# A one-core Perceiver kernel: eight key groups of its second cross-attention computed at the end of the first one, and a state-space scan whose inputs come from ScalarE and whose states TensorE adds

## The chip, the cores and the metric

The kernel runs on one core of one Trainium2 chip. The metric is the device time of one execution in microseconds. Before the change the median of 3 runs is 1534.51 us, from 1531.64 to 1535.97.

## The reference, cut to what matters

`x` is 128 rows of 256 numbers. Six layers are added to it in turn, each on the layer norm of what came before.

```python
x = x + _L0_xattn_ref(_layernorm(x), ctx_1024, Wq, Wkv, Wo, bo)     # 16 heads, 12544 context rows
x = x + _L0_attn_ref(_layernorm(x), ...)                             # banded self-attention
x = x + _L0_ffn_ref(_layernorm(x), ...)                              # 8 experts, top 2
x = x + _L1_xattn_ref(_layernorm(x), ctx_1024, mask, W, b)
x = x + _L1_attn_ref(_layernorm(x), ...)                             # scan
x = x + _L1_ffn_ref(_layernorm(x), ...)                              # 32 experts, top 8
```

The fourth layer makes its keys from the same context rows as the first, with one head, and the keys are the values too:

```python
q = relu(input @ W.T + b); k = relu(context @ W.T + b)
probs = softmax(where(mask, -inf, q @ k.T)); out = probs @ k
```

The fifth, with 256 channels and 16 states (`n`) per channel, sums over the 128 rows with cumulative sums:

```python
log_dA = clip(delta * A, -7, 20); log_R = cumsum(log_dA)
S = cumsum(delta * B * x * exp(min(-log_R, 20)))
y = sum over n of C * exp(log_R) * S, + x * D
```

## The kernel before, in words

Each layer is a stage with one instruction block per engine. Engines wait for each other through semaphores; a stage begins when every engine has left the stage before. The order on each engine is written out by hand. Layer norm is shared (`norm_vector`, `norm_pool`, `norm_tensor`, L97 to L121). `spin` (L123) issues matmuls of the identity on itself, whose result nobody reads; each float32 matmul is two MATMUL records with two weight loads.

**The context stage** (`stage_context`, L181) walks 14 chunks of 896 context rows through 16 heads: 224 steps. In step `u` TensorE turns the probabilities of head `u` (L620), turns the output of step `u - 2` (L562), on odd steps makes two heads' scores (L555), in seven of eight steps makes a value tile (L544), makes a key piece for step `u + 4` (L533) and multiplies the probabilities of step `u - 1` with the values (L575). ScalarE copies the turned probabilities (L396), then the value tile (L402), then exponentiates the next step (L378, L380). VectorE takes the low parts, maxima and running sums. GpSimd splits value tiles (L317, L318) and, once per chunk, the context chunk after next into a high float32r part and a low rest (`split_context`, L295 and L297). The last eight steps make no value tiles, the last four no key pieces. After step 223 TensorE projects the heads with `wo` (L588), in parts, since the last sums arrive last.

**The band stage** (`stage_band`, L1560) is the second layer. While it runs, SyncE loads what the later stages need (L1599 to L1613), one context chunk among it. **`stage_mix0`** (L1418) is the third: a router chain of small VectorE operations (L1459 to L1469) beside the experts on TensorE (L1531, L1540). GpSimd splits the relu stage's weight `wx` and context chunk 0 meanwhile (L1443 to L1450).

**The relu stage** (`stage_relu_context`, L1066) is the fourth. A chunk's keys are four groups: `relu_keys` (L1390) is six float32r matmuls of 448 columns (L1401) into bank `G % 2`, and ScalarE adds the bias and the relu (L1189). VectorE casts a group to its high part (L1258), GpSimd takes the low part (L1162). TensorE turns the keys (L1316), makes the scores (L1328, L1333), turns the probabilities (L1374) and sums (L1344). Group 0 to 3 are made ahead (`done = [4]`), and rounds 0 to 12 make four groups each, those of the next chunk. ScalarE splits the high part of a context chunk (L1196), GpSimd the low part (L1157). The keys `d_kT` have a ring of two chunks.

**The scan stage** (`stage_scan`, L842) works in four blocks of 64 channels by 16 states, 1024 columns. VectorE and GpSimd make the products with `ea` (L972, L909), GpSimd makes the inputs `g` (L900), TensorE takes cumulative sums with a triangle (L1044, L1053), ScalarE exponentiates (L929, L932), VectorE multiplies (L989, L996) and adds the 16 states of each channel (L997). **`stage_mix1`** (L675) is the sixth layer and begins with `spin(8, 0)`.

## Time and profile before

| | |
|---|---|
| median of 3 runs | 1534.51 us |
| the profiled execution | 1531.62 us |
| its span | 1529.9 us |
| TensorE matmuls busy | 96% |
| VectorE busy | 71% |
| ScalarE busy | 54% |
| GpSimd busy | 39% |
| mean granted clock of TensorE | 0.987 |

The profiled execution took 1.7 us more than its span, which is what lies around the instructions. Shares are means over stages with different limits. A timeline row gives the start from the span's start in us, the duration in us (of all instructions of a merged row together), the engine, the line, what is written and read, the shape, the count, and in brackets the idle time of the engine before it with what ended it. PE is TensorE, PEld its weight loads, DVE VectorE, ACT ScalarE, POOL GpSimd. A duration reported for a group counts its tail, so successive starts say better what an instruction costs in a stream.

### The profile page before, as it was taken

Reading aid. Unit: us, or ns where it says so; the run is one execution under the profiler, and the core shown is the slowest. Engines: PE = TensorE matmul, PEld = TensorE weight load, DVE = VectorE, ACT = ScalarE, POOL = GpSimd, SP = SyncE. Lnnn points to the kernel's source line nnn. Section 1 sums busy time; section 2 is a strip of 40 time slices with the busy share of each in tenths; the row PEclk is TensorE's granted clock in tenths of the full one; section 3 lists DMA queues with packets and bytes.
Section 4 is the critical chain, followed back from the end, with each engine's and each line's share of the span. In section 5 each row is a group of like instructions: output and inputs, shape, how many; then the busy total and the mean of one; then the engine's idle time right before and its main releaser. Section 6 shows DMA issues by size and latency. Waiting matters only on the chain. (4 is left out here: it accounts for less than half of the span.)

```text
span 1529.9 us, 24927 instructions
## 1 busy us (share of the span) xinstructions
PE 1467.8 (96%) x9257; PEld 1272.2 (83%) x9257; DVE 1084.1 (71%) x2051; ACT 832.6 (54%) x1581; POOL 598.7 (39%) x517
## 2 busy tenths in 40 slices
PE   8999999999999999999999999999987979999769
PEld 6888888888888888888888888888875869999648
DVE  5777777777777777777777777777787337777784
ACT  4555566556555565556656566556652136666221
POOL 5243433434343434343434343343310245666240
PEclk9999999999999999999999999999999799999899
DMA  5000000000000000000000000000004221221720
GB/s 186 1 25 1 1 25 1 25 1 25 1 25 1 25 1 25 1 25 1 25 1 20 6 1 25 1 1 1 1 28 179 83 105 55 82 82 34 302 104 4
DMA packets 11099, 58.92 MB, mean 39 GB/s; under 512 B 2330, under 2 KB 4707, under 8 KB 9956
## 3 DMA queue, kind: packets, MB, share of 16 engines
q1 hardware_dynamic: 10980, 57.33, 10.0%
q8 instruction: 75, 1.23, 0.3%
q14 instruction: 44, 0.36, 0.1%
HBM read 57.19 MB, written 0.13 MB: 37 GB/s over the span
## 5 line engine op out<-in xcount | busy, mean ns | idle before, releaser
L487 DVE TENSOR_TENSOR pT<-ps,pT 128x896 fp32r<-128x896 f32 x224 | 244.5, 1091 | 203.8 <-ACT pT L396 203.8
L317 POOL CAST V<-Vraw 128x512 fp32r<-128x512 f32 x189 | 115.7, 612 | 651.1 <-ACT Vraw L402 550.5
L396 ACT ACTIVATE pT<-ps 128x896 fp32r<-128x896 f32 x224 | 205.9, 919 | 179.4 <-PE ps L562 178.6
L402 ACT COPY Vraw<-ps 128x512 f32<-128x512 f32 x189 | 110.9, 587 | 266.0 <-PE ps L544 266.0
L318 POOL TENSOR_TENSOR V<-Vraw,V 128x512 fp32r<-128x512 f32 x189 | 242.7, 1284 | 15.1
L433 DVE TENSOR_REDUCE nmx<-ps 128x1 f32<-128x896 f32 x224 | 242.0, 1080 | 0.0
L380 ACT ACTIVATE prob<-ps,nm 128x896 f32<-128x896 f32 x224 | 223.8, 999 | 0.0
L620 PE MATMUL ps<-ident,prob 128*128 128x128 f32 x1568 | 214.2, 277 | 8.7 <-ACT prob L380 4.5
L575 PEld LDWEIGHTS ps<-pT,V 128*128 128x128 f32 x1568 | 215.0, 188 | 8.1 <-issue 0.3
L575 PE MATMUL ps<-pT,V 128*128 128x256 f32 x1568 | 220.3, 280 | 0.0
L620 PEld LDWEIGHTS ps<-ident,prob 128*128 128x128 f32 x1568 | 167.5, 140 | 17.0 <-ACT prob L380 9.2
L441 DVE TENSOR_REDUCE osb<-ps 128x128 f32<-128x256 f32 x224 | 95.0, 424 | 89.2 <-PE ps L575 80.0
L544 PE MATMUL ps<-wvh,cTh 128*128 128x512 f32 x392 | 141.8, 443 | 1.1 <-DVE V L477 1.1
L426 DVE TENSOR_TENSOR Kl<-ps,Kh 128x448 fp32r<-128x448 f32 x224 | 137.4, 614 | 1.8 <-ACT Kh L371 1.8
L533 PE MATMUL ps<-cTh,wkh 128*128 128x448 f32 x448 | 131.0, 373 | 6.5 <-DVE Kl L426 2.3
L533 PE MATMUL ps<-cTh,wkl 128*128 128x448 f32 x448 | 128.4, 368 | 0.5 <-DVE wkl L464 0.5
L533 PE MATMUL ps<-cTl,wkh 128*128 128x448 f32 x448 | 128.2, 367 | 0.4 <-DVE cTl L461 0.4
L544 PE MATMUL ps<-wvh,cTl 128*128 128x512 f32 x392 | 123.1, 395 | 0.0
L544 PE MATMUL ps<-wvl,cTh 128*128 128x512 f32 x392 | 122.6, 394 | 0.0
L371 ACT CAST Kh<-ps 128x448 fp32r<-128x448 f32 x224 | 118.5, 529 | 1.7 <-PE ps L533 1.5
L533 PEld LDWEIGHTS ps<-cTh,wkh 128*128 128x128 f32 x448 | 81.5, 188 | 30.8 <-DVE Kl L426 12.7
L555 PE MATMUL ps<-Kh,qh 64*128 64x448 f32 x448 | 94.0, 415 | 0.0
(312 smaller groups left out, 2426.7 us busy)
## 6 DMA issues: line engine op xcount, KB each, us to landing
raw<-in_ctxT SPq DMA_DIRECT2D x14, 896.0 KB, 4.4
d_raw<-in_ctxT SPq DMA_DIRECT2D x14, 896.0 KB, 4.6
w<-in_w SPq DMA_DIRECT2D x2, 4096.0 KB, 18.1
wg<-in_wg SPq DMA_DIRECT2D x1, 4352.0 KB, 17.8
wu<-in_wu SPq DMA_DIRECT2D x1, 4352.0 KB, 27.6
wd<-in_wd SPq DMA_DIRECT2D x1, 4352.0 KB, 36.3
e_ea<-in_alog SPq DMA_DIRECT2D x1, 2048.0 KB, 7.8
d_mrow<-in_mask SPq DMA_DIRECT2D x14, 112.0 KB, 4.5
```

Of the source, the lines that this page charges most:

```text
L317: link(pool, nc.gpsimd.tensor_copy(v_high(g, i), by_head(Vraw[:, j % 2, :])), "pool_chain")
L318: nc.gpsimd.tensor_tensor(v_low(g, i), by_head(Vraw[:, j % 2, :]), v_high(g, i).bitcast(F32), ALU.subtract).then_inc(sem("v_split"), 1)
L371: nc.scalar.copy(Kh[:, slot, cols], ps[:, piece_bank(p), 0:HK]).then_inc(sem("kh_ready"), 1)
L380: nc.scalar.activation(prob[:, :, :], S[u % 2], ACT.Exp, bias=nm[:, par, h:h + 1], scale=1.0, accum_out=rs[:, b:b + 1]).then_inc(sem("exp_ ...
L396: nc.scalar.activation(pT[u % 2][:, :, 0, :], pT_ps, ACT.Copy).then_inc(sem("pTh_ready"), 1)
L426: nc.vector.tensor_tensor(Kl[:, slot, cols], ps[:, piece_bank(p), 0:HK], Kh[:, slot, cols].bitcast(F32), ALU.subtract).then_inc(sem("kl_re ...
L433: nc.vector.tensor_reduce(nmx[:, :], S[u % 2], mybir.AxisListType.XY, ALU.max, negate=True).then_inc(sem("chunk_max"), 1)
L487: nc.vector.tensor_tensor(pT[u % 2][:, :, 1, :], pT_ps, pT[u % 2][:, :, 0, :].bitcast(F32), ALU.subtract).then_inc(sem("pTl_ready"), 1)
L533: mm = nc.tensor.matmul(ps[:, piece_bank(p), 0:HK], w[:, k, m * P:(m + 1) * P], x[:, k, half * HK:(half + 1) * HK], start=(n == 0), stop=( ...
L544: mm = nc.tensor.matmul(ps[:, bank, :], x[:, k, i * P:(i + 1) * P], w[:, k, cols], start=(n == 0), stop=(n == 3 * KT - 1))
L575: mm = nc.tensor.matmul(OT_ps, V[g % 2][:, k, h % HG, :], pT[u % 2][:, k, :, :].rearrange("p a q -> p (a q)"), start=(k == 0), stop=(k == ...
L620: mm = nc.tensor.transpose(pT_ps[:, k, :], prob[:, :, :].rearrange("p a n -> p (a n)")[:, k * P:(k + 1) * P], ident[:, :])
```

## The change

It does these things:

- **Context stage.** SyncE loads `wx` into the first half of the value buffer and GpSimd splits it near the start. SyncE loads context chunks 0 and 1 once more after chunk 13; GpSimd splits the first as any chunk (at step 206) and the second in quarters after all value splits. In steps 216, 217, 218, 219, 222 and 223 TensorE makes one relu key group each in bank 6, and ScalarE relus it between the copy of the turned probabilities and the next exponential. Groups 6 and 7 follow in banks 2 and 3 amid the final projection.
- **Buffers.** `row0` and `dist` leave the lasting buffers; `tri` and `below` are made in `stage_mix0`; the `afc` load moves to the band stage. The key ring is four chunks, its first two shared with the context stage and with the scan.
- **Band and mix0.** Three runs of `spin(3, ...)` are added between the last matmuls of the band; the first spin of `stage_mix0` goes from 8 to 6. Context chunks 2 and 3 are loaded in the band stage, 4 and 5 in `stage_mix0`, whose GpSimd splits 2 and 3. VectorE's router selection waits for `below`.
- **Relu stage.** It starts at group 8, groups 8 to 12 are made ahead, rounds 0 to 8 make three groups, rounds 9 to 12 four. Chunk 0's casts come ahead of the query's, and its key turns ahead of groups 10 to 12.
- **Scan.** GpSimd makes three `ea` products instead of two and no inputs. ScalarE makes all inputs with 16 instructions of 256 elements, each written with a step of 16 elements. VectorE makes one product and no state sums; TensorE adds the states of a block with 16 matmuls of the identity on 64 columns that lie 16 elements apart, at the end.
- **mix1.** The first spin goes from 8 to 5.

```diff
+                def later_keys(G, bank):
+                    act.wait_ge(sem("dk_done"), G + 1)
+                    act.wait_ge(sem("wx_early"), 32)
...
@@ stage_context, TensorE @@
+                    if u in later_at:
+                        pe.wait_ge(sem("o_added"), u - 1)
+                        pe.wait_ge(sem("vraw_ready"), len(v_steps))
+                        later_keys(later_at.index(u), 6)
...
+                        if u in later_at:
+                            pe.wait_ge(sem("dkT_ready"), later_at.index(u) + 1)
                         weighted_sum(u - 1)
...
                         project(range(0, 4))
+                        later_keys(6, 2)
...
                 turn_heads((4, 5, 6), 7)
+                later_keys(7, 3)
@@ stage_relu_context @@
-    early, split = v["early_groups"], v["early_splits"]
-    ahead = v["groups_ahead"]
-    done = [max(early, ahead)]
+    early, done = 8, [13]
+    SKIP = 2
...
-        share = -(-(groups - done[-1]) // left) if left > 0 else 0
+        share = (groups - done[-1]) // left if left > 0 else 0
@@ stage_scan, ScalarE @@
+                for k in range(NST):
+                    ins = nc.scalar.activation(cn(g[:, :])[:, :, k], dx[:, :], ACT.Copy, scale=bc[:, k:k + 1])
+                ins.then_inc(sem("g_ready"), 1)
@@ stage_scan, VectorE @@
-                    nc.vector.tensor_reduce(y[:, n * BD:(n + 1) * BD], cn(la[n][:, :]), AX_X, ALU.add).then_inc(sem("y4_ready"), 1)
...
+                dve.wait_ge(sem("states_added"), NB)
+                nc.vector.tensor_tensor(res[:, :], res[:, :], ps[:, 0, 0:D], ALU.add).then_inc(sem("res_ready"), 1)
@@ stage_scan, TensorE @@
+                def add_states(n):
+                    pe.wait_ge(sem("y4_ready"), n + 1)
+                    pe.wait_ge(sem("neg_ready"), NB - 1)
+                    pe.wait_ge(sem("R_ready"), NB - 1)
+                    for k in range(NST):
+                        mm = nc.tensor.matmul(ps[:, 0, n * BD:(n + 1) * BD], v["ident"][:, :], cn(la[n][:, :])[:, :, k],
+                                              start=(k == 0), stop=(k == NST - 1))
+                    mm.then_inc(sem("states_added"), 1)
...
                     sums(n)
                     if n + 2 < NB:
                         log_R(n + 2)
+                    else:
+                        add_states(n - 2)
+                add_states(NB - 2)
+                add_states(NB - 1)
```

## Rows read from the trace of the kernel before

**Rows 1.** Timeline of TensorE, two successive rounds of the relu stage.

```profile
1266.67 1.07 PE L1344 MATMUL ps<-d_kNh,d_pTh 128*128 128x256 f32 x7
...
1269.26 0.57 PE L1401 MATMUL ps<-d_cTh,d_wxh 128*128 128x448 f32 x2
...
1274.13 0.92 PE L1374 MATMUL ps<-ident,d_prob 128*128 128x128 f32 x7
...
1281.65 0.63 PE L1401 MATMUL ps<-d_cTh,d_wxh 128*128 128x448 f32 x2
```

**Rows 2.** Timeline of TensorE, the relu stage before its first full round.

```profile
1240.09 0.65 PE L1401 MATMUL ps<-d_cTh,d_wxh 128*128 128x448 f32 x2
...
1249.52 0.69 PE L1316 MATMUL ps<-ident,d_kT 128*128 128x128 f32 x2 [4.50 <-DVE d_kNl L1263]
...
1259.13 0.67 PE L1401 MATMUL ps<-d_cTh,d_wxh 128*128 128x448 f32 x2 [2.06 <-ACT d_kT L1189]
```

**Rows 3.** Timeline of VectorE and GpSimd, the first chunk's casts and low parts.

```profile
1241.70 3.19 DVE L1258 CAST d_kTh<-d_kT 128x448 fp32r<-128x448 f32 x4
...
1242.16 4.80 POOL L1162 TENSOR_TENSOR d_kTl<-d_kT,d_kTh 128x448 fp32r<-128x448 f32 x4 [5.12 <-DVE d_kTh L1258]
```

**Rows 4.** Timeline of GpSimd in the context stage, around one chunk's split.

```profile
913.27 1.67 POOL L295 CAST cTh<-raw 128x1792 fp32r<-128x1792 f32 x1
...
920.85 0.61 POOL L317 CAST V<-Vraw 128x512 fp32r<-128x512 f32 x1 [1.78 <-ACT Vraw L402]
...
961.31 0.61 POOL L317 CAST V<-Vraw 128x512 fp32r<-128x512 f32 x1 [7.53 <-ACT Vraw L402]
```

**Rows 5.** Timeline of VectorE, steps 217 and 219, without value tiles.

```profile
1130.77 1.09 DVE L487 TENSOR_TENSOR pT<-ps,pT 128x896 fp32r<-128x896 f32 x1 [0.87 <-ACT pT L396]
...
1140.48 1.09 DVE L487 TENSOR_TENSOR pT<-ps,pT 128x896 fp32r<-128x896 f32 x1 [0.87 <-ACT pT L396]
```

**Rows 6.** Timeline of ScalarE and TensorE, the last two steps.

```profile
1155.46 0.28 ACT L378 ACTIVATE al<-nm 128x1 f32<-128x1 f32 x1
...
1159.53 1.99 PE L588 MATMUL ps<-wo,oT 128*128 128x256 f32 x8
...
1161.38 1.07 PE L575 MATMUL ps<-pT,V 128*128 128x256 f32 x7
```

**Rows 7.** Stretch: bounds, length, busy us per engine, clock, DMA share, GB/s.

```profile
1192.00:1196.00 4.00, 3.37 (x9) 2.28 (x10) 0.42 (x1) 0.00 (x0) 0.00 (x0) 0.50 0.47 146
```

**Rows 8.** Timeline of TensorE and VectorE in `stage_mix0`.

```profile
1197.82 3.76 PE L126 MATMUL ps<-ident 128*128 128x128 f32 x16 [0.78 <-PEq L1595]
...
1204.60 2.29 DVE L1463 TENSOR_SCALAR c_ex<-c_ex,c_one 128x8 f32<-128x8 f32 x1
...
1212.39 0.48 DVE L1481 SCALAR_TENSOR_TENSOR res<-ps,c_comb,res 128x256 f32<-128x256 f32 x1 [3.27 <-PE ps L1540]
```

**Rows 9.** Timeline of VectorE in the scan stage.

```profile
1457.38 2.94 DVE L989 TENSOR_TENSOR e_g<-e_g,e_inv 128x1024 f32<-128x1024 f32 x1
...
1473.96 1.22 DVE L997 TENSOR_REDUCE e_y<-e_la 128x64 f32<-128x1024 f32 x1
1475.21 0.42 DVE L1014 TENSOR_TENSOR res<-res,e_y 128x256 f32<-128x256 f32 x1
```

**Rows 10.** Timeline of TensorE: spins, narrow matmuls, a cumulative sum of the scan.

```profile
1178.80 2.17 PE L126 MATMUL ps<-ident 128*128 128x128 f32 x18
...
1185.49 1.93 PE L1742 MATMUL ps<-b_v,b_kx 128*128 128x16 f32 x16
...
1465.56 1.98 PE L1053 MATMUL ps<-e_g,tri 128*128 128x512 f32 x4 [1.49 <-DVE e_g L989]
```

**Rows 11.** Timeline of ScalarE in the scan stage.

```profile
1432.62 0.42 ACT L923 ACTIVATE e_u<-e_u 128x256 f32<-128x256 f32 x1 [11.59 <-DVE e_u L943]
```

**Rows 12.** Timeline of TensorE and VectorE at the start of `stage_mix1`.

```profile
1475.96 3.44 PE L126 MATMUL ps<-ident 128*128 128x128 f32 x16 [3.64 <-PEq L885]
...
1477.51 0.41 DVE L105 TENSOR_SCALAR xn<-res,mv,rstd 128x256 f32<-128x256 f32 x1 [0.66 <-POOL rstd L114]
```

More of the change, by code:

```diff
@@ L83, in build @@
         keep("ones", [P, P])
-        keep("row0", [P, P])
-        keep("tri", [P, P])
         keep("hmask", [P, HPT])
-        keep("below", [P, E1, E1])
         keep("disti", [P, 2, P], I32)
-        keep("dist", [P, P])
         keep("brow", [1, 3 * D])
-        for name in ("aq", "ak", "av", "afc"):
+        for name in ("aq", "ak", "av"):
             keep(name, [P, KT, D])
@@ L129, in build @@
         norms = (norm_vector, norm_pool, norm_tensor)
+        keep("bx", [P, KT])
+        keep("d_wxh", [P, KT, D], F32R)
+        keep("d_wxl", [P, KT, D], F32R)
+        v["d_kT"] = [sb(f"d_kT{i}", [P, KT, CK]) for i in range(2)]
         stage_context(nc, t, sb, sem, link, ps, norms, v)
+        keep("tri", [P, P])
+        keep("below", [P, E1, E1])
+        keep("afc", [P, KT, D])
+        keep("wx", [P, KT, D])
         keep("wg0", [P, KT, E0])
@@ L805, in _ @@
             def _(pe):
[L806 removed]
+                v["spin"](5, 0)
                 norm_tensor(pe, 5)
@@ L1084, in first_use @@
         return next((c for c in range(chunks) if done[c + 1] > KG * C), None)
-    to_split = {c: [C for C in range(chunks) if KG * C >= done[0] and max(first_use(C) - 1, 0) == c]
-                for c in range(chunks)}
+    to_split = {c: [C for C in range(2 + SKIP, chunks) if max(first_use(C) - 1, 0) == c] for c in range(chunks)}
     with ExitStack() as own:
@@ L1165, in _ @@
                 norm_pool(pool, 3)
-                for C in range(split, (done[0] + KG - 1) // KG):
-                    split_low(C)
                 for g in range(KG):
@@ L1209, in exp_step @@
                                          accum_out=rs[:, b:b + 1]).then_inc(sem("dexp_done"), 1)
-                act.wait_ge(sem("wx_in"), 32)
-                for C in range(split, (done[0] + KG - 1) // KG):
-                    split_high(C)
                 before = min(early + 2, done[0])
@@ L1387, in _, with relu_keys @@
                     weighted_sum(c)
-def relu_keys(nc, pe, sem, v, G, bank):
-    KG = 2 * KT
-    C, g, n = G // KG, G % KG, 0
-    m, cols = g // 2, slice((g % 2) * HK, (g % 2 + 1) * HK)
-    cTh, cTl = v["d_cTh"][C % 2], v["d_cTl"][C % 2]
-    if G >= 2:
-        pe.wait_ge(sem("dkT_ready"), G - 1)
-    pe.wait_ge(sem("dcTl_ready"), C + 1)
-    for w, c in ((v["d_wxh"], cTh), (v["d_wxl"], cTh), (v["d_wxh"], cTl)):
+def relu_keys(nc, v, g, high, low, bank):
+    m, cols, n = g // 2, slice((g % 2) * HK, (g % 2 + 1) * HK), 0
+    for w, c in ((v["d_wxh"], high), (v["d_wxl"], high), (v["d_wxh"], low)):
         for k in range(KT):
@@ L1437, in stage_mix0, with _ @@
         with nc.Block() as block:
+            @block.sync
+            def _(sp):
+                for i in range(2):
+                    sp.wait_ge(sem("dcTl_ready"), i + 1)
+                    sp.dma_start(v["d_raw"][i][:, :, :], t["ctxT"][4 + i]).then_inc(sem(f"dctx_in{i}"), 16)
             @block.gpsimd
@@ L1562, in stage_band @@
     norm_vector, norm_pool, norm_tensor = norms
-    res, xnT, ident, ones, row0, hmask, dist = (v[n] for n in ("res", "xnT", "ident", "ones", "row0", "hmask", "dist"))
+    res, xnT, ident, ones, hmask = (v[n] for n in ("res", "xnT", "ident", "ones", "hmask"))
     SCALE = DH1 ** -0.5
```

238 lines of the change are left out of this document (132 added, 106 removed).

## The prediction

> **What bounds the kernel now.** I read the page first, then the busy time by stretches, then the timelines of the stretches that the change touches. The chain of waits of the page reaches back only through the last stage, so each stage has to be read for itself. In the relu stage's rounds TensorE runs without a pause: a round is 1281.65 - 1269.26 = 12.39 us, its four key groups are the first 4.87 us, so 1.22 us a group and 0.203 us a matmul [rows 1]. In the context stage without value tiles two steps take 9.71 us, and VectorE's row shows it waiting for ScalarE, so that the chain copy, exponential, low part is as long as TensorE's work [rows 5]. In the scan VectorE is the bound: its rows follow each other, and where one is longer than its twins it waited for GpSimd [rows 9]. The stage heads wait for one engine after another, and TensorE's clock falls there: 0.50 of full speed, the 1.2 GHz level, in the stretch after the band's 16-column matmuls [rows 7, 10].
>
> The sum is made against the profiled execution, 1531.62 us, 1.7 us more than its span. The median of the runs is 2.9 us above it; I apply the same change to it.
>
> **Context stage, eight groups added.** *Start.* The load and split of `wx` stand on SyncE's and GpSimd's queues ahead of chunk 1's split, 2 us of GpSimd; `row0`, `tri` and `below` leave the same queue, and GpSimd waits for ScalarE's first value tile after them: nothing. If that slack were gone it would cost 2 us once. *Chunk 14's split at step 206.* After an earlier chunk's split (1.67 us cast, then the rest) GpSimd still waited 1.78 us for ScalarE [rows 4]: nothing; without that cover, up to its own 6 us. *Groups 0 to 3, steps 216 to 219.* Eight steps with seven value tiles take 961.31 - 920.85 = 40.46 us [rows 4], without tiles 4 x 9.71 = 38.84 [rows 5], so a tile of six 512-column matmuls costs 0.23 us of time, not its 1.3 of TensorE. The bounds for a group are 0 and its full 1.22; I take 0.25, the nearest row, and 1.0 for the four. *Group 4, step 222.* The relu stands on ScalarE between the copy and the exponential, which start 0.0 us apart today [rows 6]. The six matmuls start with the copy and need 1.25, the copy is over after 0.8, the relu adds 0.6: the exponential of the last step is 1.05 late, and the last probabilities with it. *Group 5, step 223.* TensorE is now the late one: 1.22, and the weighted sum waits for the relu in its bank, 0.75: 1.97. *Group 6.* L588 runs straight into the next rows [rows 6]: 1.22. *Group 7.* Before the last turn TensorE idles about 0.3 today: 0.95. *Quarters.* GpSimd's eight pieces hold up VectorE's small operations with two SBUF operands: 0 to 2, I take 0.5. Together **+6.7**, bounds +3 (groups 4 to 7 half hidden) and +10.
>
> **Band and mix0.** The three added spins fill TensorE's idle pieces while VectorE copies. Bounds: the clock stays at half as now, and each spin of 0.7 us outlasts its wait a little, +0.5; or it is back at the 2.4 GHz level before the band's last projection, -4.5. The old stream at half clock was 16 spins in 3.76 us [rows 8] against 18 in 2.17 [rows 10], and those spins held the turned norm up by 1.3. With 12 spins at full clock that 1.3 goes, and some 1.7 of norm, logits and first expert at half clock. With 12 at half clock 0.9 goes. I take -3.0, since the stretch is nearly gapless with the spins. Against it: GpSimd now works until about 1213 instead of 1207. VectorE's L1463, 8 elements wide, took 2.29 us because GpSimd held it up [rows 8]. The router's later operations will be caught the same way by chunk 3's cast and its 4 us rest, so the weights of the experts come some 6 us later. They were idle for 3.27 before first use [rows 8], and TensorE waits for the first addition only two experts on, so of the 6 I leave 0.9 on the path; bounds 0 and 3. Together **-2.1**. The late `afc` load is the first in its queue and needed 25 us later: nothing.
>
> **Relu stage.** *Head.* Old: last key turn at 1249.52 after 4.50 idle, third group of round 0 at 1259.13 [rows 2]. New: chunk 0 is there, so after the query's projection (1240.09, where group 2 began) TensorE has turns and scores, 12.39 - 4.87 - 2.6 (sum, from 1266.67) - 0.9 (probabilities) = 4.0, and groups 10 to 12, 3.65: 1247.7. The casts and low parts, 3.19 and 4.80 [rows 3], begin 2.6 earlier and are done. From the last turn to the third group 9.61 were needed [rows 2], with 12 score matmuls at half clock in it (4.9), which now come before: 4.7. One more us for the last copy and low part: third group of round 0 at 1253.3. That is 5.8 earlier, and the fourth group is gone, 1.2: **-7.0**. *Rounds 1 to 8.* Eight groups less, 9.8 us of TensorE. Casts no longer wait for ScalarE, and run as in rows 3: 5.3 us from the first cast to the last low part. They start about 1.8 us into a round and TensorE asks for them at 7.1, so they are just in time. ScalarE's high split stands ahead of the probabilities' copy and can cost 0.2. Bounds 0 and 9.8; I take 1.1 each, **-8.8**. Rounds 9 to 12 keep four groups and their time.
>
> **Scan.** VectorE loses one product and four sums of 1.22 us [rows 9], and two waits for GpSimd's inputs of about 1.7 each (2.94 against 1.22). By the same order of work the third cumulative sum, 1465.56 [rows 10], starts 6.3 us earlier: 1459.2. From there TensorE is the bound. A float32 matmul is two instructions. They cost 2.17 / 18 = 0.12 us at 128 columns and 1.93 / 16 = 0.12 at 16 [rows 10], so 64 columns between them cost 0.12 as well, and a block's 16 matmuls 16 x 2 x 0.115 = 3.7. The order is sum, states, sum, states, states, states: 2 x 1.85 + 4 x 3.7 = 18.5, end at 1477.7, and 0.5 for the addition: 1478.2 against 1475.63: **+2.6**. ScalarE's inputs: 16 x 0.33 to 0.42 [rows 11] are 5.3 to 6.7, from 1439.8; the first exponential that stands behind them is due at 1449.4: nothing, up to 0.6 each. Beyond that each 0.1 costs 1.6.
>
> Both new accesses go in steps of 16 elements, and no row shows such a step. If TensorE read it at a quarter of its rate, a 64-column pass would take four times 1.98 / 4 x 64 / 512, 0.25 instead of 0.12; at half rate it hides. The Trainium skill, Advanced Engine Details and Errata, section SBUF Cachelines, says that lines are 16 bytes and that an access which meets a new line each time pays a penalty; these steps are 64 bytes, so by it the states cost more than rows 10 give. No run here shows it yet. I take no penalty, since the nearest rows leave half the time of a pass free.
>
> **mix1.** `xn` is there at 1477.92, the 16 spins last until 1479.40 [rows 12]. Ten at full clock, which the states keep up, take 1.2 us: the norm goes when `xn` does, 1.2 earlier, and 0.2 for the clock: **-1.4**. With a cold clock 0.3 is left.
>
> Sum: 6.7 - 2.1 - 7.0 - 8.8 + 2.6 - 1.4 = -10.0. The profiled execution would be 1521.6, the median **1524.5 us**.
>
> **Rivals.**
> 1. *Strided access is slow (slower than before).* In the scan, as above, at a quarter of the rate: TensorE's 128 state instructions go from 0.115 to 0.22 or more, +13.5; ScalarE's inputs at four times 0.33 take 21 us, the first exponential waits until 1461, and the whole of what follows is 11 late. +24.5 on the forecast, less than 3 of it hidden: 1546. It decides from half the rate on. For: no row excludes it, and the page speaks for it. Against: only the free half. Chance 0.07. With TensorE alone slow it is 1538, no change: 0.04.
> 2. *The rounds don't shorten.* VectorE, GpSimd and ScalarE form a loop of about 11 us a round; if casts wait behind the long low parts, a round stays at 12.4. +8.8: 1533. For: GpSimd has four low parts (4.8) and in most rounds a 4 us rest, with VectorE's casts between. Against: rows 3 give the four casts and low parts in 5.3. Chance 0.08.
> 3. *The early groups are paid in full.* If relus and quarter splits stall each of the last steps, context +10 and the head gains half: 1531. Chance 0.05, on the border of no change.
> 4. *All hides.* Context +3, clock -4.5, scan 0, rounds -9.8: 1514. Chance 0.12. That the early groups are computed and save nothing isn't among them: the groups of the relu stage are counted.
>
> The forecast, 1517 to 1530, has 0.64. Low 1512, high 1533. A change within 0.3%, 4.6 us, is about what a measurement of this kernel can't tell from none. Faster by more than that: 0.64 + 0.12, and 0.04 of rivals 2 and 3, which lie at the border, 0.80; no change: their other 0.09 and the 0.04 of TensorE alone, 0.13; slower 0.07.
>
> **What would show it.** Relu: 48 groups; rounds 0 to 8 at 11.3 us and 9 to 12 at 12.4, TensorE without a pause; the third group of round 0 6 us nearer to the stage's start. Context: `res` 6 to 7 us later than 1166.1. Clock above 0.50 between the band's end and the first expert. Scan: 128 matmul records of the states at 0.115 us from start to start, VectorE idle in the last 8 us. Wrong if the states' records lie further apart, if ScalarE's inputs end after 1449, or if a round with three groups has an idle piece over 0.5 us.

## The result, and the profile after the change

The changed kernel takes 1526.72 us in the median of 5 runs (1520.80 to 1526.90), against 1534.51 us before (5 runs, 1531.64 to 1537.58). The ratio is 0.994, with a 95% interval of 0.9924 to 0.9955. The interval leaves out 1, so it is faster, by 7.8 us and well under 1%; 10.0 were forecast. The profiled execution is the median one, 1526.72 us with a span of 1524.3 us, 4.9 us under the profiled execution of before; the spans differ by 5.6.

`res` is written once at the end of each stage, so the distances between these rows cut both profiles into stages without a remainder. The context stage is cut once more, at the low part of the chain copy in step 215, the last step before the new groups. Times in us:

| stretch | before | after | difference | forecast |
|---|---|---|---|---|
| start to step 215 | 1120.86 | 1119.04 | -1.8 | 0 |
| step 215 to `res` (context) | 45.26 | 50.74 | +5.5 | +6.7 |
| band | 30.95 | 33.74 | +2.8 | with mix0 -2.1 |
| mix0 | 37.77 | 38.14 | +0.4 | |
| relu | 190.63 | 176.12 | -14.5 | -15.8 |
| scan | 49.74 | 53.26 | +3.5 | +2.6 |
| mix1, to the end | 54.69 | 53.26 | -1.4 | -1.4 |

The rows follow in the order of the forecast's steps. First the last two steps of the context stage, TensorE's timeline, with groups 4 and 5 (L1442), the weighted sums (L609) and group 6:

```profile
1153.38 0.64 PE L1442 MATMUL ps<-cTh,d_wxh 128*128 128x448 f32 x2
...
1155.56 1.09 PE L609 MATMUL ps<-pT,V 128*128 128x256 f32 x7 [0.72 <-ACT d_kT L408]
...
1157.58 0.65 PE L1442 MATMUL ps<-cTh,d_wxh 128*128 128x448 f32 x2
...
1159.77 1.09 PE L609 MATMUL ps<-pT,V 128*128 128x256 f32 x7 [0.72 <-ACT d_kT L408]
...
1163.05 0.76 PE L1442 MATMUL ps<-cTh,d_wxh 128*128 128x448 f32 x2
```

Each weighted sum waits 0.72 us for the relu in its bank, as the forecast had it (0.75). On ScalarE the relu of group 4 (L408) stands ahead of the last exponential (L399 begins it):

```profile
1154.87 0.63 ACT L408 ACTIVATE d_kT<-ps,bx 128x448 f32<-128x448 f32 x1 [0.36 <-PE ps L1442]
1155.40 0.28 ACT L399 ACTIVATE al<-nm 128x1 f32<-128x1 f32 x1
```

The band, TensorE's timeline, and the granted clock (the figure ahead of the last two) in two stretches:

```profile
1186.57 1.09 PE L1787 MATMUL ps<-ident,b_s 128*128 128x128 f32 x8 [1.85 <-ACT b_s L1752]
1188.24 1.97 PE L1787 MATMUL ps<-ident,b_s 128*128 128x128 f32 x8 [0.58 <-ACT b_s L1752]
1190.00 6.85 PE L1794 MATMUL ps<-b_v,b_kx 128*128 128x16 f32 x32
1196.68 1.63 PE L122 MATMUL ps<-ident 128*128 128x128 f32 x6
```

```profile
1188.00:1190.00 2.00, 1.76 (x9) 1.76 (x9) 1.97 (x2) 1.09 (x2) 0.00 (x0) 0.50 0.91 393
...
1200.00:1202.00 2.00, 2.00 (x12) 1.88 (x11) 0.42 (x1) 0.00 (x0) 0.00 (x0) 0.68 0.18 45
```

The clock is at 0.50, the 1.2 GHz level, from the second half of the first transposes on, behind 1.85 and 0.58 us of idle time. So the 16-column matmuls, 1.93 us for 16 at the upper level [rows 10], take 6.85 for 32. The added spins (L122) come only after that. Behind them the clock is back at its upper level, and the first spins of mix0 run at it (12 in 1.58 us; 16 took 3.76 before [rows 8]):

```profile
1204.27 1.58 PE L122 MATMUL ps<-ident 128*128 128x128 f32 x12 [0.78 <-PEq L1646]
```

In mix0 VectorE's router, held up by GpSimd's two splits instead of one:

```profile
1210.07 3.87 DVE L1512 TENSOR_SCALAR c_ex<-c_ex,c_one 128x8 f32<-128x8 f32 x1
...
1215.78 3.90 DVE L1453 TENSOR_TENSOR c_ties<-c_ties,below 128x64 f32<-128x64 f32 x1
...
1221.29 0.48 DVE L1531 SCALAR_TENSOR_TENSOR res<-ps,c_comb,res 128x256 f32<-128x256 f32 x1
```

The relu stage, TensorE's timeline of its head and of one round:

```profile
1254.39 0.38 PE L1358 MATMUL ps<-ident,d_kT 128*128 128x128 f32 x2
...
1259.93 1.12 PE L1442 MATMUL ps<-d_cTh,d_wxh 128*128 128x448 f32 x2 [2.72 <-ACT d_kT L1237]
...
1262.34 1.70 PE L1421 MATMUL ps<-ident,d_prob 128*128 128x128 f32 x7
...
1275.07 0.93 PE L1421 MATMUL ps<-ident,d_prob 128*128 128x128 f32 x7
...
1286.26 0.93 PE L1421 MATMUL ps<-ident,d_prob 128*128 128x128 f32 x7
```

The third group of round 0 comes 18.3 us after the stage's start (1241.66), where it came 24.3 after it before [rows 2]. It waits 2.72 us for ScalarE, and runs at half clock. The turned probabilities (L1421) mark the rounds: 11.19 us here, 78.67 / 7 = 11.24 from 1275.07 to 1353.74, against 12.39 [rows 1]; the four rounds with four groups take 12.48.

The scan, TensorE's timeline, then VectorE's and ScalarE's rows:

```profile
1444.19 3.39 PE L1098 MATMUL ps<-e_g,tri 128*128 128x512 f32 x4 [3.11 <-DVE e_g L1035]
...
1453.03 1.98 PE L1098 MATMUL ps<-e_g,tri 128*128 128x512 f32 x4 [0.30 <-DVE e_g L1035]
1454.85 3.71 PE L1107 MATMUL ps<-d_kT,ident 128*128 128x64 f32 x32
1458.39 1.92 PE L1098 MATMUL ps<-e_g,tri 128*128 128x512 f32 x4
1460.14 3.72 PE L1107 MATMUL ps<-d_kT,ident 128*128 128x64 f32 x32
1463.68 7.32 PE L1107 MATMUL ps<-e_la,ident 128*128 128x64 f32 x64
```

```profile
1449.33 1.23 DVE L1029 TENSOR_SCALAR e_inv<-ps 128x1024 f32<-128x1024 f32 x1 [1.30 <-PE ps L1089]
...
1471.04 0.42 DVE L1059 TENSOR_TENSOR res<-res,ps 128x256 f32<-128x256 f32 x1 [9.47 <-PE ps L1107]
```

```profile
1432.20 8.24 ACT L970 ACTIVATE e_g<-e_dx,e_bc 128x256 f32<-128x256 f32 x16 [1.93 <-DVE e_dx L1013]
```

A state instruction costs (1458.39 - 1454.85) / 32 = 0.111 us: the 64 columns that lie 16 elements apart cost what narrow matmuls cost [rows 10]. From the third cumulative sum (1453.03) to `res` are 18.0 us of TensorE's work, and VectorE is idle for the last 9.47, while its four sums were 1.22 each [rows 9]. The first weighted sum waits 3.11 us for VectorE and takes 3.39 instead of 1.98, since it begins at half clock.

### The profile page after: what moved, and what is told of

Same layout as the page of the kernel before. It is cut to its first block and busy times, and to the rows that moved or that the text cites. A ratio compares the mean times of both kernels' runs of the same rounds, so it can differ in the third digit from the quotient of the medians.

```text
span 1524.3 us, 25220 instructions
## 1 busy us (share of the span) xinstructions
PE 1479.7 (97%) x9393; PEld 1291.9 (85%) x9393; DVE 1068.4 (70%) x2046; ACT 835.9 (55%) x1594; POOL 600.4 (39%) x521
## 5 line engine op out<-in xcount | busy, mean ns | idle before, releaser
L609 PEld LDWEIGHTS ps<-pT,V 128*128 128x128 f32 x1568 | 215.0, 188 | 10.3 <-ACT d_kT L408 2.2
L609 PE MATMUL ps<-pT,V 128*128 128x256 f32 x1568 | 220.2, 280 | 1.4 <-ACT d_kT L408 1.4
```

The costliest lines, as they stand in the source:

```text
L609: mm = nc.tensor.matmul(OT_ps, V[g % 2][:, k, h % HG, :], pT[u % 2][:, k, :, :].rearrange("p a q -> p (a q)"), start=(k == 0), stop=(k == ...
```

## The experiments

Stage lengths of every profile, in us, with the median of its runs. The ratio given with each run is to the kernel before on the same chip. A, B and C are the theories of the text that stands ahead of each result, written before the run.

| kernel | context | band | mix0 | relu | scan | mix1 | median |
|---|---|---|---|---|---|---|---|
| before | 45.26 | 30.95 | 37.77 | 190.63 | 49.74 | 54.69 | 1534.5 |
| before_again | 45.26 | 34.99 | 35.69 | 192.31 | 51.40 | 54.98 | 1534.5 |
| after | 50.74 | 33.74 | 38.14 | 176.12 | 53.26 | 53.26 | 1526.7 |
| scan_old | 50.75 | 31.74 | 36.51 | 174.90 | 50.86 | 55.89 | 1522.0 |
| scan_vsum | 52.30 | 31.69 | 35.89 | 174.77 | 47.20 | 57.80 | 1520.8 |
| relu_head | 51.09 | 31.68 | 35.89 | 172.06 | 51.88 | 53.25 | 1517.5 |
| scan_contig | 50.72 | 30.11 | 35.88 | 174.88 | 54.73 | 53.24 | 1520.8 (1 run) |
| band_nospin | 50.77 | 31.25 | 37.56 | 174.83 | 54.77 | 53.27 | 1524.2 |
| spins_more | 50.74 | 31.72 | 35.89 | 175.23 | 52.09 | 53.28 | 1520.5 |
| ctx_one | 50.07 | 32.76 | 35.90 | 174.77 | 51.90 | 53.64 | 1520.6 (1 run) |
| ctx_banks | 49.47 | 30.13 | 35.90 | 174.88 | 54.70 | 54.83 | 1524.5 |
| comb1 | 52.30 | 31.70 | 35.90 | 172.01 | 45.09 | 53.06 | 1512.4 |
| comb2 | 49.12 | 31.75 | 35.89 | 172.10 | 43.93 | 53.07 | 1507.2 |
| comb3 | 49.12 | 28.59 | 34.32 | 172.18 | 43.94 | 53.02 | 1503.4 |

In the profiles in which these stages have the code of after, the band differs by up to 3.6 us (30.1 to 33.7) and the scan by 2.9 (51.9 to 54.8): these are the places where TensorE's clock falls in one execution and not, or later, in another. A stage is compared with these spreads in mind, and effects are read from rows.

### The scan as before

```diff
@@ GpSimd @@
+                inputs(0)
...
-                for n in range(1, NB):
+                for n in range(2, NB):
...
+                inputs(1)
...
+                    if n + 2 < NB:
+                        inputs(n + 2)
@@ ScalarE @@
-                for k in range(NST):
-                    ins = nc.scalar.activation(cn(g[:, :])[:, :, k], dx[:, :], ACT.Copy, scale=bc[:, k:k + 1])
@@ VectorE, outputs(n) @@
+                    nc.vector.tensor_reduce(y[:, n * BD:(n + 1) * BD], cn(la[n][:, :]), AX_X, ALU.add).then_inc(sem("y4_ready"), 1)
@@ TensorE @@
-                    else:
-                        add_states(n - 2)
-                add_states(NB - 2)
-                add_states(NB - 1)
```

> The scan alone goes back to the old division of work: GpSimd makes the inputs of each block, VectorE makes two products and adds the 16 states of every block, TensorE adds none. Everything else is the changed kernel. Theory A (in the changed scan TensorE is the bound from the third cumulative sum on, and its 128 state instructions cost more than VectorE's four sums did): the stage from one addition to res to the next goes from 53.3 us back to 49.7, the run is 3 to 4 us faster than the changed kernel, about 1523. Rival B (the scan is longer only because a cumulative sum fell into a stretch of half clock): the stage stays at 52 to 53, within 1 us of the changed kernel. By my prediction's term it would be 2.6 us faster.

Measured: 1522.0 us, ratio to before 0.9917 (0.9889 to 0.9945). The scan takes 50.86, between the 49.74 and 51.40 of the two profiles of before and under all of the changed code. A holds for the stage. But mix1 takes 55.89, as before the change or more: its matmuls begin at half clock. The two stages together take 106.75, against 106.52 after. So the run's 4.7 us under after are not the scan's: band, mix0 and the relu stage were shorter in this profile, by 4.9 together, with the code of after. The intervals of the two ratios overlap.

### VectorE adds the states at the end

```diff
@@ VectorE; add_states(n) is its tensor_reduce of block n, TensorE has none @@
                 outputs(NB - 2)
+                add_states(0)
                 outputs(NB - 1)
+                for n in range(1, NB):
+                    ins = add_states(n)
```

> The changed scan keeps ScalarE's inputs, but VectorE adds the states, block 0 while it waits for the last cumulative sum and blocks 1 to 3 behind the last product; TensorE adds none. Theory A (ScalarE's inputs are the good half of the change and the states on TensorE the bad half): VectorE is free at 1457.7 after the third product; one sum of 1.22 us, the last product of 1.21 and three more sums follow each other, so res is written at 1463.9 instead of 1471.0: 7 us faster than the changed kernel, about 1519.7. Rival B (TensorE's states only fill time in which the last cumulative sum or ScalarE would have been waited for): the last product comes no earlier than 1460.4, and with three sums behind it res is at 1465.6 or later, 5 us or less. Rival C (without the states TensorE is idle for more than 5 us and the next stage begins at half clock): 2 us of the gain are lost in the next stage.

Measured: 1520.8 us, ratio 0.9905 (0.9886 to 0.9923). VectorE's timeline, and TensorE's at the start of mix1:

```profile
1455.30 1.21 DVE L1058 TENSOR_REDUCE d_kT<-d_kT 128x64 f32<-128x1024 f32 x1
1456.57 1.23 DVE L1042 TENSOR_TENSOR e_la<-ps,e_R 128x1024 f32<-128x1024 f32 x1
...
1461.20 0.42 DVE L1066 TENSOR_TENSOR res<-res,d_kT 128x256 f32<-128x256 f32 x1
```

```profile
1461.95 2.48 PE L122 MATMUL ps<-ident 128*128 128x128 f32 x10 [5.66 <-PEq L937]
```

The scan is 47.20: 6.1 shorter than after, and 7.5 shorter than in band_nospin and ctx_banks, which like it have a first sum of 3.78 us. So A is right on the stage, and C on the rest: TensorE was idle for 5.66 us, the ten spins take 2.48 us instead of the 1.35 of after, and mix1 is 57.80 instead of 53.26. That is a loss of 4.5 where C had 2. The same row of after:

```profile
1471.79 1.35 PE L122 MATMUL ps<-ident 128*128 128x128 f32 x10 [0.78 <-PEq L937]
```

What TensorE's states gave was the clock of the next stage.

### Two relus ahead of the first exponential

```diff
                 rows_high(0, 3)
+                for G in range(done[0], done[0] + 2):
+                    keys(G)
                 exp_step(0)
...
-                    for G in range(done[c], done[c + 1]):
+                    for G in range(done[c] + (2 if c == 0 else 0), done[c + 1]):
```

> On ScalarE the relus of the first two key groups of round 0 move from behind the first exponential to ahead of it. Nothing else. Theory A (TensorE's 2.72 us of idle time before the third group come from ScalarE's order, and the half clock from 1259 to 1267 comes from that idle time): the third group starts at 1257.1 instead of 1259.9 and the clock stays at its upper level, so 2.8 and some 2 to 3.5 us more are won, 1521 to 1522. Rival B (the exponential comes late by the relus and TensorE waits for it instead): TensorE is idle for 1 to 2 us one group later, the clock falls all the same, and the gain is 1 us or less.

Measured: 1517.5 us, ratio 0.9888 (0.9865 to 0.991). TensorE's timeline:

```profile
1254.13 0.57 PE L1444 MATMUL ps<-d_cTl,d_wxh 128*128 128x448 f32 x2
1255.67 0.98 PE L1423 MATMUL ps<-ident,d_prob 128*128 128x128 f32 x7 [0.98 <-ACT d_prob L1255]
```

The third group follows the second without a pause, and the first turned probabilities come 17.8 us after the stage's start instead of 20.7. The stage is 172.06, 4.1 under after and 2.8 under the other profiles of the same code, whose clock fell less. A holds: 2.9 us are the pause that is gone (the third group comes 15.4 us after the stage's start instead of 18.3). The clock stayed at its upper level, but that gave some 1.2 us here and not the 2 to 3.5 expected; the two parts can't be divided exactly, since in the other profiles the clock fell too, for a shorter time. The rest of the 9.2 us between the two medians is not this edit's stage.

### The same counts on elements that lie together

```diff
-                    ins = nc.scalar.activation(cn(g[:, :])[:, :, k], dx[:, :], ACT.Copy, scale=bc[:, k:k + 1])
+                    ins = nc.scalar.activation(g[:, k * D:(k + 1) * D], dx[:, :], ACT.Copy, scale=bc[:, k:k + 1])
...
-                        mm = nc.tensor.matmul(ps[:, 0, n * BD:(n + 1) * BD], v["ident"][:, :], cn(la[n][:, :])[:, :, k],
+                        mm = nc.tensor.matmul(ps[:, 0, n * BD:(n + 1) * BD], v["ident"][:, :], la[n][:, k * BD:(k + 1) * BD],
```

> Leaves the right order of the states out: ScalarE writes its 16 inputs as 16 blocks of 256 elements that lie together, and TensorE reads 64 elements that lie together for each state matmul, so wrong elements are added; the counts and sizes are those of the changed kernel. Theory A (TensorE's state matmuls are bound by their weight loads and instructions, not by how the 64 columns are read): 0.111 us from record to record as before. Rival B (steps of 16 elements cost TensorE something): 0.06 to 0.09. For ScalarE: if the step of its writes costs nothing, 16 inputs take 8.2 us again; if it does, they take 16 x 0.42 = 6.7 or less. The time stays within 1 us of the changed kernel under A.

Measured, TensorE's and ScalarE's timelines:

```profile
1449.71 3.68 PE L1107 MATMUL ps<-d_kT,ident 128*128 128x64 f32 x32
1453.23 1.94 PE L1098 MATMUL ps<-e_g,tri 128*128 128x512 f32 x4
```

```profile
1425.56 6.50 ACT L970 ACTIVATE e_g<-e_dx,e_bc 128x256 f32<-128x256 f32 x16 [1.96 <-DVE e_dx L1013]
```

TensorE: 3.52 / 32 = 0.110 us, the same. ScalarE: 0.41 an instruction instead of 8.24 / 16 = 0.515, so its steps of 64 bytes cost 0.11 us, a quarter. The Trainium skill, Advanced Engine Details and Errata, section SBUF Cachelines, names a penalty for accesses that each meet a different line. The rows show one for ScalarE's writes, and none for TensorE's reads of 64 columns. Whether there is none, or one that fits into what such an instruction costs anyway, they don't show: 16 and 128 columns take 0.12 us too [rows 10]. The 1.7 us on ScalarE are off the path: TensorE's wait for the first input is 3.11 us, as in after.

### The band without its spins, and with more of them

In band_nospin the three added `spin(3, ...)` of the band go, and `stage_mix0` begins with `spin(8, 3)`. The edit of spins_more:

```diff
@@ stage_band @@
-                v["spin"](9, 7)
+                v["spin"](16, 7)
                 for h in range(H1):
+                    if h == HPT:
+                        v["spin"](2, 7)
@@ stage_mix0 @@
-                v["spin"](6, 3)
+                v["spin"](10, 3)
@@ stage_scan @@
-                v["spin"](5, 4)
+                v["spin"](17, 4)
```

> The changed kernel without the three spins between the last matmuls of the band, and with 8 instead of 6 in the first spin of stage_mix0: that part of the change undone. Theory A (my prediction's term: the spins hold the clock): band and mix0 together take 3 us more, or more than that. Theory B (the clock falls before them, in TensorE's 1.85 us of idle time ahead of the band's first transposes and in the 16-column matmuls, so they can only bring it back sooner): band shorter by up to 1 us, mix0 longer by 1 to 2, together within 1 us of the changed kernel. Stage lengths of the changed kernel, from its profiles so far: band 30.1 to 33.7, mix0 35.9 to 38.1.

> The changed kernel with TensorE's idle time filled at four places: 16 instead of 9 ahead of the band's first transposes (1.85 us idle), 2 new ones amid them (0.58), 10 instead of 6 at the start of stage_mix0 (1.24), 17 instead of 5 ahead of the scan's first weighted sum (3.11). Theory B (the clock falls because of these pauses): the granted clock stays at its upper level from 1170 to 1250, band 29.5 to 30.5 and mix0 35 to 36, the scan's first weighted sum takes 1.98 instead of 3.4 to 3.8 and VectorE's wait of 1.3 to 2.8 us behind it goes, scan 1.3 to 2.5 shorter than 51.9 to 53.3; together 3 to 6 us, 1521 to 1523. Rival (spins of the identity weigh nothing for the clock, or the 16-column matmuls pull it down whatever is ahead of them): the clock falls in the band all the same, and the gain there is under 0.5.

Measured: band_nospin 1524.2 us, ratio 0.9928 (0.9911 to 0.9945), band 31.25 and mix0 37.56, together 68.8; seven profiles with the three spins have 66.0 to 71.9, in the mean 68.0. Theory A's 3 us are not there, so B holds: without them mix0 is 1.7 longer than the usual 35.9 and the band no longer. The first spins of mix0:

```profile
1202.81 3.75 PE L122 MATMUL ps<-ident 128*128 128x128 f32 x16 [0.78 <-PEq L1646]
```

In all three profiles without the added spins (before, before_again, band_nospin) these run at half clock, 16 in 3.75 or 3.76 us, and in none of the eleven with them. So the added spins do bring the clock back ahead of mix0. What that is worth in sum, 0.8 us by these means, isn't shown: it lies inside the spread, and the median without the spins, 1524.2, is no slower than the 1526.7 with them.

spins_more: 1520.5 us, ratio 0.9903 (0.9885 to 0.9922). TensorE's timeline in the band and in the scan:

```profile
1187.39 1.09 PE L1789 MATMUL ps<-ident,b_s 128*128 128x128 f32 x8 [0.29 <-ACT b_s L1752]
...
1190.05 1.93 PE L1796 MATMUL ps<-b_v,b_kx 128*128 128x16 f32 x16
1192.63 2.36 PE L1796 MATMUL ps<-b_v,b_kx 128*128 128x16 f32 x16 [0.65 <-DVE b_kx L1731]
...
1440.04 1.98 PE L1098 MATMUL ps<-e_g,tri 128*128 128x512 f32 x4 [0.41 <-DVE e_g L1035]
```

In the scan the first sum takes 1.98. By itself that decides nothing, since relu_head and ctx_one have 1.98 behind the full pause of 3.11 us, as here in relu_head:

```profile
1436.38 1.98 PE L1098 MATMUL ps<-e_g,tri 128*128 128x512 f32 x4 [3.11 <-DVE e_g L1035]
```

But of the seven profiles with that pause five have the sum slowed by the clock (3.39 to 3.78 us), and of the four with 17 spins (this one, comb1, comb2, comb3) none. That speaks for B there without proving it; the stage's 52.09 is no less than the 51.9 of the two that kept the clock anyway. In the band the clock fell all the same, but late in the 16-column matmuls, and the band stayed at 31.7: the rival is not excluded there. The band's gain was below what was expected.

### One matmul instead of six in each early group

```diff
-                    relu_keys(nc, v, G % LG, cTh[c % 2], cTl[c % 2], ps[:, bank, 0:HK]).then_inc(sem("dk_done"), 1)
+                    g = G % LG
+                    nc.tensor.matmul(ps[:, bank, 0:HK], v["d_wxh"][:, 0, (g // 2) * P:(g // 2 + 1) * P],
+                                     cTh[c % 2][:, 0, (g % 2) * HK:(g % 2 + 1) * HK], start=True,
+                                     stop=True).then_inc(sem("dk_done"), 1)
```

> Leaves five of the six matmuls of each of the eight early key groups out, so the first two chunks' keys of the relu stage are wrong; semaphores, relus, loads and splits stay. From step 215's chain copy to the context's addition to res the kernel before took 45.3 us and the changed one 50.7 to 52.3. Theory A (TensorE's matmuls are the cost, as in my prediction for groups 4 to 7): 46 to 47. Rival B (the relus between copy and exponential and GpSimd's split in quarters are the cost): 49 or more. Groups 0 to 3 alone, to step 219's row: 19.6 before, 20.3 changed; under A 19.7.

Measured: 1520.6 us, one run. TensorE's timeline of step 222:

```profile
1154.24 0.44 PE L623 MATMUL ps<-cTh,d_wxh 128*128 128x448 f32 x1
1155.95 1.09 PE L609 MATMUL ps<-pT,V 128*128 128x256 f32 x7 [1.27 <-ACT d_kT L408]
```

From step 215 to 219 it took 19.65 us, as before the change (19.62; after 20.28): there the matmuls are the whole cost, 0.6 us for four groups. To `res` it took 50.07: B. The wait for the relu only grew, from 0.72 to 1.27; besides, the clock fell around 1149 and in the projection, so the last part can't be divided exactly. What GpSimd's split in quarters costs, the other half of B, no run shows by itself.

### Other banks, and everything together

The edit of ctx_banks on ScalarE; TensorE writes to the same banks, and its weighted sums wait for the relus of groups 0 to 3 alone:

```diff
-                    if u in later_at:
+                    if u in later_at[0:4]:
                         later_keys(later_at.index(u), 6)
                     if u + 1 < steps:
                         exp_step(u + 1)
+                    if u in later_at[4:]:
+                        later_keys(later_at.index(u), 1 + u - (steps - 2))
...
-                later_keys(6, 2)
+                later_keys(6, 3)
...
-                later_keys(7, 3)
+                later_keys(7, 1)
```

comb1 is relu_head and spins_more, and in the scan `add_states(0)` on TensorE behind the last sum, blocks 1 to 3 on VectorE as in scan_vsum. comb2 adds ctx_banks and, on TensorE:

```diff
@@ stage_context @@
+                    if u == steps - 3:
+                        pe.wait_ge(sem("kl_ready"), steps)
+                        v["spin"](6, 7)
+                    if u == steps - 2:
+                        pe.wait_ge(sem("pTl_ready"), u)
+                        v["spin"](6, 4)
@@ stage_band @@
+                    if h == 8:
+                        v["spin"](2, 7)
@@ stage_scan @@
+                    else:
+                        half = NST // 2
+                        add_states(0, range((n - 2) * half, (n - 1) * half))
+                pe.wait_ge(sem("y4_ready"), NB - 1)
+                v["spin"](11, 4)
```

comb3 adds to that, on GpSimd in `stage_mix0`:

```diff
                 norm_pool(pool, 2)
+                pool.wait_ge(sem("xn_ready"), 3)
...
+                pool.wait_ge(sem("comb0_ready"), 1)
                 for i in range(2):
```

> The changed kernel with groups 4 to 7 in other banks of PSUM: group 4 in bank 1, group 5 in bank 2, group 6 in bank 3, group 7 in bank 1 again, so that the weighted sums of the last two steps no longer wait for the relus; and on ScalarE the relu of group 4 stands behind the last exponential instead of ahead of it. The run ctx_one showed that without the matmuls step 222 costs the same 0.7 us. Theory A (the relus and the waits for them are what the last steps pay): TensorE's two waits of 0.72 us go, the last exponential starts 0.6 earlier, and from step 215's chain copy to res it takes 48.7 to 49.5 us instead of 50.7; 1.2 to 2 us in all. Theory B (TensorE's own 1.2 us a group are the bound there): 50.2 or more, gain under 0.5.

> Three things together: the relus of round 0's first two groups ahead of the first exponential; the longer spins of the run spins_more; and in the scan TensorE adds the states of block 0 alone, while VectorE adds those of blocks 1 to 3. Expected from the stages: relu 172 instead of 175 to 176, scan 53.3 - 7 - 1 - 1.5 = 44 to 45 (in scan_vsum it was 47.2), and the last stage at full clock because TensorE's state matmuls end within 1 us of res (53.3 instead of the 57.8 of scan_vsum), band and mix0 as in spins_more. Together 1526.7 - 4 - 8.5 - 3 = 1511. Rival: the clock falls at another place, as it did in scan_vsum, and the sum is 1515 or more.

> comb1 with four additions: the banks of ctx_banks; 6 spins each ahead of the turned probabilities of steps 221 and 222, where TensorE was idle for 1.7 to 2.1 and 1.8 us; 2 spins between the two halves of the band's 16-column matmuls (0.65 idle); in the scan half of block 0's state matmuls ahead of the last cumulative sum, where TensorE was idle for 1.90 us and the clock fell, and 11 spins behind the other half. Expected: context 48.5 to 49.5 from step 215 (comb1 52.3, where the clock had fallen in these pauses), band 30 (31.7), scan 44 (45.1), mix0, relu and the last stage as in comb1 (35.9, 172.0, 53.1). Together 4 to 6 us under comb1: 1507. Rival (a fall of the clock only moves to the next pause, such as the band's first matmuls): 2 us or less under comb1.

> comb2 with GpSimd's work in stage_mix0 moved: tri and below are made once xn is written, and the splits of context chunks 2 and 3 only after the router's weights (comb0_ready). Tests the prediction's term of 0.9 us for VectorE's router operations that GpSimd holds up. In comb2 the router took VectorE from 1205.8 to 1218.3, three of its operations 1.7 to 4.0 us instead of about 0.2, TensorE waited 0.77 us for the first addition, and xn took 1.27 instead of 0.67. Theory A: xn 0.6 sooner, the router done in 3 to 5 us, TensorE's wait gone, mix0 34.5 instead of 35.9; the splits are done before the relu stage asks for them: 1.4 us, 1505.8. Rival B: the later splits are late for the first keys of the relu stage, or end the cover of something else: stage relu longer than 172.1 by what mix0 wins.

ctx_banks: 1524.5 us, ratio 0.9944 (0.993 to 0.9957), which can't be told from the changed kernel. But the context's end takes 49.47, 1.3 less, although the clock fell in it, and the waits for the relu are gone: A. Bank and order were changed together, and no run has one of them alone.

comb1: 1512.4 us, ratio 0.9856 (0.9833 to 0.9879). Its scan is 45.09 and mix1 53.06: with 3.7 us of state matmuls TensorE bridges VectorE's sums, and both gains hold. The context took 52.30, because the clock fell after the pauses of steps 221 and 222 (0.63 from 1152 to 1156).

comb2: 1507.2 us, ratio 0.9829 (0.9816 to 0.9843): the context 49.12, the scan 43.93, the band no better. Its router, VectorE's timeline, GpSimd's rest of a chunk at the first of the two, and TensorE's wait behind the router; then VectorE's rows of comb3:

```profile
1207.07 4.01 DVE L1473 TENSOR_TENSOR c_wins<-c_ex 128x64 f32<-128x64 f32 x1
...
1212.73 4.02 DVE L1475 TENSOR_TENSOR c_ties<-c_ties,below 128x64 f32<-128x64 f32 x1
```

```profile
1207.02 3.97 POOL L1521 TENSOR_TENSOR d_cTl<-d_raw,d_cTh 128x1792 fp32r<-128x1792 f32 x1
```

```profile
1219.00 1.97 PE L1612 MATMUL ps<-w,c_hT 128*128 128x256 f32 x8 [0.77 <-DVE res L1553]
```

```profile
1202.83 0.22 DVE L1473 TENSOR_TENSOR c_wins<-c_ex 128x64 f32<-128x64 f32 x1
...
1208.81 0.48 DVE L1555 SCALAR_TENSOR_TENSOR res<-ps,c_comb,res 128x256 f32<-128x256 f32 x1 [3.78 <-PE ps L1614]
```

comb3: 1503.4 us, ratio 0.9801 (0.9776 to 0.9825), the fastest kernel here: 31 us under before, where the change gave 8. With GpSimd out of the way an operation takes 0.22 us instead of 4.01, mix0 is 34.32, 1.6 less, and the relu stage is no longer for it (172.18): A. In its profile the clock stayed up through the whole band, which is then 28.59. The band's code is that of comb2, whose profile has 31.75, so these 3.2 us are the spread between executions and not the edit's.

### The kernel before once more

> The kernel before, unchanged, for a second profile of it: whether its stages are the same each time. Context to step 215's chain copy 1120.9 in the first profile, 1119.0 to 1120.1 in eleven profiles of changed kernels. Theory A (the change makes these 1.2 us): 1120.9 again within 0.3. Rival B (executions differ by that much): 1119 to 1120.5. Band and mix0 were 30.95 and 37.77, with TensorE at half clock from 1189 to 1206; if the place where the clock falls moves from execution to execution, band is longer by 1 to 3 and mix0 the same or shorter.

Measured: 1534.5 us, ratio 1.0003. TensorE's timeline in the band:

```profile
1187.29 6.85 PE L1742 MATMUL ps<-b_v,b_kx 128*128 128x16 f32 x32
```

Step 215's row is at 1120.67 us, against 1119.0 to 1120.1 in twelve profiles of changed kernels: A, on two profiles of before. The changed code comes 0.6 to 1.8 us sooner there, gathered evenly over the chunks; why is open. In the band it is B: this time the clock fell where it fell in the profile after, and the band took 34.99 us instead of 30.95.

## Why the prediction was right, and where it was not

The time, the sign and the largest term came out as forecast, inside the range. That the sum came as near as it did is in part luck: in the profile the band and mix0 missed by 5.3 us, and 1.8 came back at the start, where nothing was forecast.

- *Relu stage, -15.8 forecast, -14.5 in the profile, -15.4 to -15.9 in seven other profiles with its order.* The rounds that lose a group went from 12.48 to 11.24, 1.24 each where 1.1 was taken, so rival 2 fell. The first of them, in part at half clock, saved nothing (12.73 against 12.46). The four rounds that keep four groups kept their 12.5, which shows that the saving is the group's. The second profile of before has 1.7 us more in this stage, so against it the saving is 16.2. The head's third group was forecast 18.5 us after the stage's start and came at 18.3. From the last turn to the third group 5.7 us were forecast and 5.5 came, so the wait in it was carried over rightly. What it is made of was not asked: ScalarE has the relus of round 0 behind the first exponential, and relu_head won the 2.72 us back. And the clock that falls in the wait stood at nothing: the third group took 2.4 us instead of 1.2, which is what the fourth one had saved. So the head gave 6.1 us up to the first turned probabilities, where 7.0 were forecast.
- *Context, +6.7 forecast, +5.5.* Groups 0 to 3 cost 0.66 instead of 1.0, group 4 0.83 instead of 1.05, and the rest 4.0 instead of 4.6. Rival 3 fell. For group 4 the mechanism was the one given, the relu ahead of the exponential: ScalarE begins the last exponential 1.80 us after the copy in after (1155.40 against 1153.60) and 0.81 in comb2, where the relu stands behind it, as before the change (0.82). The steps from 219 to 223 take 18.86 us in comb2, which has other banks and spins as well, against 18.66 before and 19.49 after. The quarters' 0.5 no run shows by itself.
- *Scan, +2.6 forecast, +3.5.* The states came as the forecast's count said: 18.0 us from the third sum to the start of the addition, where the sum had 18.5. Rival 1 fell with scan_contig. The third sum came 4.8 earlier, not 6.3 (the parts named there, one product, two waits and the one sum that lies ahead of it, give 5.9). TensorE came through the second decay sum and its spins sooner, while VectorE still had the skip product of 2.15 us ahead of the first input, so TensorE's pause before the first sum grew from 1.42 to 3.11 us, and in this profile the sum ran at half clock. The pause by itself cost nothing: in relu_head and ctx_one it is as long, the sum runs at the upper level, the third sum comes 6.2 earlier and the stage is 51.9. So "by the same order of work" held, and what the step had at nothing is the clock. Over the five profiles with the scan of after the mean is 53.3, over the two of before 50.6: +2.7. ScalarE's inputs cost 0.515 each, above the 0.33 to 0.42 taken, and stayed hidden.
- *Band and mix0, -2.1 forecast, +3.2 in the profile.* This is the term that failed in size. It rested on one profile of before, in which the clock fell at 1189, after the first 16-column matmuls. In before_again the two stages take 70.7 instead of 68.7, and in seven profiles of changed code 66.0 to 71.9, in the mean 68.0: 1.7 less than the mean of before. So the mean is near the forecast, but not for the reason given, and that is luck: -3.0 was to come from the spins, whose worth the runs put at 0.8 us and don't show apart from the spread. The step that failed is the pair of bounds: they let the clock stay at half "as now", and not fall earlier than in the one profile. It did, before 1188, and the 16-column matmuls then took 6.85 us, as they did in before_again with no change made. The upper bound of +0.5 should have been +3. The spins did bring the clock back ahead of mix0, as forecast, but stand behind the pause in which it falls. The router's 0.9 was 0.77 or 0.78 in the eight profiles of that order in which mix0 took 35.9, and nothing in after, scan_old and band_nospin, where TensorE was slower.
- *mix1, -1.4 forecast, -1.4.* In ctx_banks the same code took 54.83, 1.6 more than here.
- *The start, 0 forecast, -0.6 to -1.8:* outside every step, and its cause is open. It is also part of why `res` of the context came 3.7 us later and not the 6 to 7 named as a sign.

The profiled executions differ by 4.9 us and the medians by 7.8, because the profiled execution of before lay 2.9 us under its median; the second one lay 2.5 over it.

## What to carry to other kernels

Work moved onto TensorE at the end of a stage can pay through the clock of the next stage and lose as work; here it was enough to give TensorE what bridges the pause (one block of four, in comb1). When one engine of a chain is made faster, look at which pause grows: here two grew, from 2.06 [rows 2] to 2.72 us and from 1.42 to 3.11. The first cost its own length and some 1.2 us by the clock; the second cost nothing by itself, and 1.4 to 2.9 where the clock fell behind it. Where relus and an exponential share an engine, try both orders before counting matmuls: behind it won in the context stage (there in another bank as well), ahead of it at the head of the relu stage. And profile the kernel before more than once: two profiles of it differ by 4.0 us in the band, which is half of what the whole change gave.

## What the runs showed of the hardware

- Reading the moving operand in steps of 64 bytes cost TensorE nothing that shows at 64 columns of float32 (0.110 us in one piece, 0.111 in steps); writing in such steps cost ScalarE 0.11 us on 0.41 for 256 elements.
- VectorE's operations of 64 elements took 4.0 us instead of 0.2 beside GpSimd's 4.0 us rest of a chunk. The Trainium skill, SBUF — State Buffer, section Terms, says that of the two engines on the shared port pair "the loser **fully blocks**"; by that rule the whole of GpSimd's operation is waited for, and the rows agree: in comb2 GpSimd's operation runs from 1207.02 to 1210.99, VectorE's from 1207.07 to 1211.08.
- The same program loses its clock at different places from execution to execution: the band took 30.95 and 34.99 us in two profiles of the same kernel. Whether filling the pauses makes it steadier is open: comb2's four runs lie within 1.9 us and comb1's four, with fewer pauses filled, within 7.5; but comb3's four, filled as comb2's, lie within 3.6, and nine of the kernel before on comb2's chip within 4.4.
